# Attention softmax on score rows: one score product instead of two, exponentials in place, probabilities transposed by TensorE

## The reference

```
x = x + tanh(g_xattn) * attention(layernorm(x), ctx, mask)
    Q, K, V = projections, Q and K rotated (RoPE)
    scores  = Q K^T / sqrt(32);  scores = -inf where mask == 0
    out     = softmax(scores) V, heads joined, times W_o
x = x + tanh(g_ffn) * experts(layernorm(x))
    affinity = softmax(x gate^T);  each of 8 experts takes its top 56 rows of every batch
    out = scatter-add of gating * down(silu(gate(x)) * up(x))
```

## Time and profile before

| | us |
|---|---|
| median of 3 runs (1951.43 to 1954.47) | 1953.86 |
| profiled execution | 1952.03 |
| its span | 1950.1 |
| TensorE busy | 1816.3 (93%) |
| VectorE busy | 1020.4 (52%) |
| ScalarE busy | 717.0 (37%) |
| GpSimd busy | 213.3 (11%) |
| mean granted TensorE clock | 0.970 |

### The profile page before, as it was taken

The page is one execution under the profiler, slowest core; times in us unless marked ns, Lnnn a source line. Parts: engine busy times, 40 slices in busy tenths (PEclk is TensorE's granted clock), DMA queues, the critical chain, the costliest instruction groups (busy, mean ns, idle before and its releaser), DMA issues. The chain is left out here.

```text
span 1950.1 us, 30053 instructions
## 1 busy us (share of the span) xinstructions
PE 1816.3 (93%) x11654; PEld 1564.5 (80%) x11654; DVE 1020.4 (52%) x1650; ACT 717.0 (37%) x1134; POOL 213.3 (11%) x288
## 2 busy tenths in 40 slices
PE   7999974999999999998299999999999999999995
PEld 6989962776676676775189999999999999999995
DVE  6665643676676576574444353543535445354441
ACT  3232221444344444353044343433424334343340
POOL 0000001112122112111100020200202011020101
PEclk9999996999999999999689999999999999999998
DMA  5545446565465564551333353533535334353431
GB/s 221 192 172 204 159 151 159 135 166 140 123 171 139 125 177 134 128 152 39 113 105 109 98 147 116 137 108 99 154 108 137 114 108 136 108 145 108 120 105 19
DMA packets 77229, 257.33 MB, mean 132 GB/s; under 512 B 10824, under 2 KB 10824, under 8 KB 75856
## 3 DMA queue, kind: packets, MB, share of 16 engines
q1 hardware_dynamic: 65136, 221.92, 37.1%
q0 software_dynamic: 12000, 34.13, 7.4%
HBM read 193.39 MB, written 51.61 MB: 126 GB/s over the span
## 5 line engine op out<-in xcount | busy, mean ns | idle before, releaser
L1413 PE MATMUL gu_ps<-xs_hi,ws_hi 128*128 128x448 f32 x1024 | 372.4, 364 | 3.0 <-DVE xs_lo L1348 3.0
L1415 PE MATMUL gu_ps<-xs_hi,ws_lo 128*128 128x448 f32 x1024 | 371.9, 363 | 0.0
L1414 PE MATMUL gu_ps<-xs_lo,ws_hi 128*128 128x448 f32 x1024 | 371.0, 362 | 0.0
L786 DVE CUSTOM_DVE_ANT_0 junk<-m_ps,mq 112x752 f32<-112x752 f32 x256 | 236.1, 935 | 198.0 <-PE m_ps L1047 195.7
L1343 DVE TENSOR_TENSOR ws_lo<-w_raw,ws_hi 128x1024 fp32r<-128x1024 f32 x192 | 235.4, 1226 | 189.1 <-ACT ws_hi L1293 188.1
L671 ACT ACTIVATE e_t<-s_ps 125x448 f32<-125x448 f32 x384 | 201.1, 547 | 221.7 <-PE s_ps L1074 221.1
L1293 ACT ACTIVATE ws_hi<-w_raw 128x1024 fp32r<-128x1024 f32 x192 | 201.7, 1051 | 164.4 <-PE y_ps L1432 146.6
L1413 PEld LDWEIGHTS gu_ps<-xs_hi,ws_hi 128*128 128x128 f32 x1024 | 192.7, 188 | 15.4 <-issue 3.3
L1414 PEld LDWEIGHTS gu_ps<-xs_lo,ws_hi 128*128 128x128 f32 x1024 | 192.6, 188 | 13.5
L1415 PEld LDWEIGHTS gu_ps<-xs_hi,ws_lo 128*128 128x128 f32 x1024 | 192.8, 188 | 13.2
L1074 PE MATMUL s_ps<-qs,ks 128*125 128x224 f32 x768 | 197.8, 353 | 0.0
(11 more groups left out here) (133 smaller groups left out, 2552.0 us busy)
## 6 DMA issues: line engine op xcount, KB each, us to landing
w_raw<-wstream SPq DMA_DIRECT2D x192, 512.0 KB, 3.5
ks<-k_split SPq DMA_DIRECT2D x192, 188.0 KB, 3.8
k_split<-k_split SPq DMA_DIRECT2D x32, 752.0 KB, 3.5
v_rows<-v_out SPq DMA_DIRECT2D x16, 750.0 KB
vs<-v_rows SPq DMA_DIRECT2D x16, 750.0 KB
c_raw<-ctxT SPq DMA_DIRECT2D x7, 1500.0 KB, 12.9
qs<-q_hi POOLq DMA_DIRECT2D x64, 112.0 KB, 3.0
mq_raw<-maskq SPq DMA_DIRECT2D x8, 656.2 KB, 10.3
```

What stands on the lines that cost most here:

```text
L786: nc.vector.tensor_tensor_reduce(junk[u % 2][:].rearrange("p (a n) -> p a n", a=2), m_ps[u % 2][0:QP, :, 0:KN], mq[:, qc].rearrange("p (a ...
L1413: nc.tensor.matmul(o, w_hi[s][:, w], xs_hi[:, c], start=(c == 0), stop=False)
L1414: nc.tensor.matmul(o, w_hi[s][:, w], xs_lo[:, c], start=False, stop=False)
L1415: mm = nc.tensor.matmul(o, w_lo[s][:, w], xs_hi[:, c], start=False, stop=(c == DC - 1))
```

## The change

The second score product is gone. VectorE's instruction keeps what it used to throw away: it writes the masked scores, times minus the scale, to `sm` and their row minimum to `least`. ScalarE takes the exponential of these rows in place in SBUF, with `least` as the bias, and its instruction sums the row into `sums`. TensorE transposes the probabilities of a head (12 transposes, four for each of three PSUM tiles), and ScalarE or, in 8 of the 48 tiles of a batch, VectorE copies a tile to `e_t`. The reciprocal is now taken of 8 sums a row; GpSimd spreads it over 32 columns each, TensorE turns that, ScalarE copies it, and VectorE multiplies straight from PSUM. The matmuls with ones, the transposed mask with its load and conversion, and the extra rows of `qs` and `ks` go. The scores run three heads ahead.

TensorE's new parts, and its order in a head t:

```
-                    nc.tensor.matmul(o, identb[0:KP, 0:KP], mt[j][:, 2 * pc:2 * pc + 2, :].rearrange("p c s -> p (c s)"), start=True, stop=False)
...
+                def turn_rows(b, h, pc):
+
+                    if pc == 0:
+                        for qc in range(QC):
+                            pe.wait_ge(exp_done[qc], H * b + h + 1)
+                    n = tile_of(b, h, pc)
+                    if n >= 2:
+                        pe.wait_ge(*emptied(n - 2))
...
+                            mm = nc.tensor.transpose(t_ps[n % 2][0:KP, a:a + QP], sm[:, h % SR, qc, c * KP:c * KP + KP], ident[0:QP, 0:QP])
...
+                def turn_parts(b, q):
+
+                    after(pe, cx_done, NG * b + q)
+                    pe.wait_ge(spread_done, NG * b + q + 1)
...
+                        turn_rows(b, t, 0)
+                        next_scores(0)
+                        turn_rows(b, t, 1)
+                        next_scores(1)
+                        if t % HG:
                             last_values()
+                        turn_rows(b, t, 2)
+                        if t % HG == 0:
+                            last_parts()
```

ScalarE's:

```
+                    nc.scalar.activation(rows, rows, ACT.Exp, bias=least[:, h % KSLOTS, qc:qc + 1], scale=-1.0,
+                                         accum_out=sums[:, h // HG % 2, qc, h % HG:h % HG + 1]).then_inc(exp_done[qc], 1)
...
                         for pc in range(KC // 2):
+                            if not on_dve(t, pc):
+                                empty(b, t, pc)
+                            if pc < QC:
+                                next_exp(pc)
+                            if pc == 0 and t % HG == 1:
+                                if t > HG:
+                                    copy_parts(b, t // HG - 1)
...
+                        if t == 8 and not last:
+                            high_q(b + 1)
```

VectorE's, and the first lines of GpSimd's:

```
+DVE_SLOTS = (0, 1, 2, 4, 7, 9, 11, 13)
...
+                                mask_scores(b, t + MLEAD, qc)
...
+                            if qc == 0 and on_dve(t, DVE_TILE):
+                                empty(b, t, DVE_TILE)
+                        if t % HG == 0:
+                            if t >= 2 * HG:
+                                normalise(b, t // HG - 2)
...
+                        if t % HG == HG - 1:
+                            invert(b, t // HG)
...
+                        if t % HG == HG - 1:
+                            spread_parts(b, t // HG)
```

More of the change, by code:

```diff
@@ L405, in attend @@
         q_hi, q_lo = sb(st, "q_hi", [P, NG, S], F32R), sb(st, "q_lo", [P, NG, S], F32R)
[L406 to L407 removed]
+        sm = sb(st, "sm", [QP, SR, QC, SK])
+        least, sums = sb(st, "least", [QP, KSLOTS, QC]), sb(st, "sums", [QP, 2, QC, HG])
+        parts, spread = sb(st, "parts", [QP, 2, QC * HG]), sb(st, "spread", [QP, 2, QC, P])
         e_t = [sb(st, f"e_t{j}", [KP, KC // 2, PAIR]) for j in range(2 * HG)]
[L409 removed]
+        c_r, cx = sb(st, "c_r", [P, S]), sb(st, "cx", [P, NG, S])
         x2 = x_res
@@ L473, in hold @@
                 def hold(s_, v_):
-                    if not (isinstance(v_, int) and v_ <= 0):
+                    if v_ > 0:
                         sp.wait_ge(s_, v_)
@@ L625, in end @@
                 def end():
-                    for q in range(1, NG):
-                        normalise(B - 1, q)
                     root(B - 1, 1, 2 * B)
@@ new lines, in next_exp @@
+                        def next_exp(qc):
+                            if t + 1 < H:
+                                exp(b, t + 1, qc)
+                            elif not last:
+                                exp(b + 1, 0, qc)
+                        for pc in range(KC // 2):
+                            if not on_dve(t, pc):
[5 more added lines that the diff above has]
+                                    copy_parts(b, t // HG - 1)
+                                elif not first:
+                                    copy_parts(b - 1, NG - 1)
+                            if pc == 0 and t in (1, 2) and not last:
+                                x_columns(b + 1, t - 1)
+                            if pc == 0 and t in (12, 13) and not first:
@@ L716, in body @@
                                 x2_columns(b - 1, t - 12)
-                            if t == 15:
-                                logit_exp(b - 1)
+                        if t == 8 and not last:
+                            high_q(b + 1)
+                        if t == 15 and not first:
+                            logit_exp(b - 1)
                 def end():
-                    for q in range(2, NG):
-                        copy_ctx(B - 1, q)
+                    copy_parts(B - 1, NG - 1)
@@ L958, in end @@
                     b = B - 1
-                    for q in range(1, NG):
-                        invert(b, q)
+                    for q in (NG - 2, NG - 1):
+                        normalise(b, q)
                     residual(b, 0)
@@ L1176, in end @@
                     b = B - 1
-                    for part in range(HG):
+                    turn_parts(b, NG - 1)
+                    for part in range(HG - 1):
                         values(b, NG - 1, part)
```

342 lines of the change are left out of this document (121 added, 221 removed).

## The result

The changed kernel takes 1978.15 us (median of 4 runs, 1977.59 to 1979.66), against 1952.64 of the kernel before on the same chip (1950.43 to 1954.47): a ratio of 1.0132, 95% interval 1.0115 to 1.015, or 25.5 us slower. I forecast 1960 and slower, so the sign is right and the size (+6) is a quarter of what it should be. The time lies inside the range of 1912 to 1985, but above the 1948 to 1975 that I gave the walk itself, and I had "slower" at 0.49 only: the sign was close to a toss. Its profiled execution has a span of 1975.7 against 1950.1, at a mean granted clock of 0.959 against 0.970.

The account below looks back on a forecast made before the run. TensorE was taken to bound the kernel before. Six full batches at +2.6 us (+16), start -2, last batch -6 and last projection -2 made +6 on 1952.03: 1958, as median 1960; range 1912 to 1985.

Parts of the forecast that it names:

- the walk: Head-by-head timing of one attention batch across the engines: 75.9 us, 76.9 with small gaps, against 74.3 before.
- rival 2: TensorE bounds the attention batches throughout: 63.6 us a batch, 1880 us in all, chance 0.12.
- the gap of 1: Small TensorE idle gaps in a batch that the head-by-head timing leaves out: 1 us added to 75.9.
- the normalise: VectorE's product that TensorE waits for in heads 0, 4, 8 and 12: 4.5 us a batch together.
- the stall of the norm: Before head 15's norm, VectorE waits for GpSimd's parts copy and then the root: 2 us a batch.
- `high_q`: ScalarE's copy at the end of head 8, which VectorE's `low_q` waits for: 1 us a batch lost.
- the values behind `copy_parts`: Value matmuls of heads 1, 5, 9 and 13 wait for ScalarE's output copy: late by 0.7 us.
- all-or-nothing rival: TensorE's clock falls to 1.2 GHz between the projections: +16 us a batch, some 2060 us, chance 0.06.
- Rival 3: ScalarE's exponential costs 1.05 us instead of 0.80: +2.5 us a batch, 1980 us, chance 0.13.
- The start: Before the full batches, three heads of maxima are needed instead of five: 2 us less.
- The last batch: No masks or scores for a next batch, so no lag there: 6 us less.
- The last projection: The final output projection follows its values sooner, where it ran at a clock of 0.50: 2 us less.

Follow-up runs that it names:

- all_three: The changed kernel with VectorE's normalise ahead of the masks, GpSimd's root ahead of the spread copy, and ScalarE's copy_parts ahead of tile copy and exponential: 1913.42 us.
- before_few_ones: The kernel before, with the matmuls with ones kept for the last of six key chunks only, so row sums omit the other five: 1921.19 us.
- norm_first: The changed kernel with VectorE's normalise (product into cx) ahead of the two masks and tile copy in heads 0, 4, 8 and 12: 1958.25 us.
- norm_copy: all_three without root_first, so VectorE's norm still waits for the root behind the spread copy: 1933.69 us.
- all_high: all_three with high_q and low_q moved from the end of head 8 to the end of head 7: 1905.40 us.
- norm_root: all_three without moving ScalarE's copy_parts: 1943.41 us.
- no_read: The changed kernel with exponentials that give no row sums (sums a constant, output unnormalised), so no accumulator reads: 1964.89 us.
- root_first: The changed kernel with GpSimd taking the root of the next batch's moments before it spreads the parts in head 15: 1969.41 us.
- filler4: The changed kernel with four extra 128x512 matmuls into an unused bank ahead of turn_parts in head 0 of six batches: 1978.20 us.

## Why the prediction was right in sign and short in size

**What bounds.** TensorE's sum fell, but to 65.65 us a batch, not 61.4; at a held clock it is 64.1 (all_three). before_few_ones shows that the engines behind TensorE were close: even without new work for them only half of what is removed comes back. So rival 2, in which all that TensorE loses comes off the time, was out of reach with the order as it is. VectorE (49.1 forecast, 48.6 measured) and ScalarE (about 50; 52.2) came out near their sums, and so did the small prices: the product 0.39 us, not 0.35, the reciprocal 0.20, not 0.17, the spread copy 0.40, not 0.5.

**The walk.** It held well. Head 14 to 0: forecast 13.9, measured 13.80. Heads 8 to 13: 24.05 and 24.99. Heads 1 to 7: 37.9 and 40.01, of which 0.8 is the fall of 3.4 us in heads 0 to 2. With the gap of 1 the walk gave 76.9; the measured 78.8 less 0.8 is 78.0, and all batches but the first, less their falls, take 77.7 to 78.0. So the walk was about 1 us a batch short. No head is off by more than 0.6 us; heads 3, 10 and 11, for which I had ScalarE's exponentials bound, take 3.50, 3.57 and 3.51, not 3.15, 3.25 and 3.2. The places at which I said the cover is lost are those that the experiments found: the normalise (norm_first: waits of 60.7 us down to 11.6), the stall of the norm (2 forecast; 1.76 measured, 1.8 a batch by norm_copy against all_three) and `high_q` (1; all_high: 1.5 a batch); and the values behind `copy_parts`, which the walk had at 0.7, waited 1.03 in head 9.

**The step that failed is the clock.** I priced it as an all-or-nothing rival (the clock at 1.2 GHz between the projections, 2060, chance 0.06) and left it out of the sum. It falls once or twice in a batch for 3.4 or 6.8 us. The short fall costs 0.8 us in heads 0 to 2 and 1.7 in the q projection of head 4, which then takes 4.89 us instead of 3.21; the long one costs 2.1 in heads 0 to 2 and 2.6 in norm_copy. The batches of 81 us have a short one in head 14 and a long one in head 0, that of 79.3 two short ones, the others one. The deficit of 18.8 us is an upper bound. Holding each of the nine falls against the same heads of a batch without one gives some 12 us in all (an estimate from the starts of the heads in the trace), of 25.5 measured against 6 forecast. The prediction called itself wrong if the granted clock left 1.00 inside the loop; on this point it was wrong, and the row for it was in my hands: 3.14 us of idling, then 0.50, while the walk had TensorE idle for over 4 us in head 0. It would have priced the five falls there, not the four behind waits of 1.5 to 1.8 us. All_three has the same transposes at a clock of 1.00 throughout the six batches, and before_few_ones, which has only the few of the kernel before, has three falls behind waits of 1.9 to 2.1 us. So the rule on transposes that I quoted from the Trainium skill ("TensorE: Matmul & The Clock Gate", Part 4: PE-mode transpose) is not enough to bring a fall about here, and not needed for one. Whether transposes make the clock fall behind shorter waits is not shown: the kernel before waited 1.34 us in every batch and kept 1.00, norm_root had falls behind waits of 0.7 and 0.8.

**The exponential.** I took 0.80; it is 0.91 from start to start, 0.81 without the sum (no_read). The Trainium skill's figure for the bias ("ScalarE: Activation LUTs", What ACT_TABLE_LOAD costs; by it I had estimated 0.82) fits the latter; the read of the accumulator costs 0.10 more. Rival 3 gives the measured total, 1980, by a price (1.05) that the trace does not show: the right number for a wrong reason. The read reaches the end with 1.2 us a batch, inside the gaps that I allowed.

**The ends.** The six batches cost +30.7, not +16: 15 more, some 12 for the falls and the rest for the walk. The start gave 4.4, not 2. The last batch was to give 6 and gave nothing: from the last mask conversion to the last output projection it takes 91.53 us, before 91.59. The last projection was to give 2 by a warm clock and did not:

```profile
950.34 5.45 PE L979 MATMUL w_ps<-wo_sb,cx 128*112 128x512 f32 x8 [0.60 <-DVE cx L764]
```

5.45 us, 5.35 before. The clock was down there again, to 0.50 from 943.7 to 954.0, so the warm clock that I had priced was not there; and the last batch has a fall of 6.8 us too, at 875.4. So of the 19.6 us that the sum was short, the batches make 14.7 and the two ends 7.3 more, less the 2.4 that the start gave beyond its 2.

**What stays open.** What exactly lets the clock fall. The wait ahead of it is part of it, since taking waits away ended the falls; but root_first shortened the longest wait and had more deficit, norm_root kept all of it with waits of 0.7 to 1.2 us while all_three has waits of 1.2 us and no fall, filler4 only moved the falls, and in norm_copy the same wait had a fall in one batch and none in another. How the 65 us of all_three divide between the clock and the waits themselves is not measured either.

## What to carry to other kernels

When a change takes work from the engine that bounds, walk the new order head by head: the lengths of the heads where no fall hit them, could be read off it to 0.6 us each before anything ran. Each wait then has two prices, its own length and what a clock that falls behind it costs; look in the trace before for a place where the engine idles that long, price the clock from there, and count on some falls behind shorter waits. Small reorderings are to be tried together: here three of them gave 44 us by themselves and 65 as a set, and turned a loss of 25 us into a gain of 39.

## What the runs showed of the hardware

An exponential that also sums its row (112x752) is followed by a read of the accumulator of 194 ns, of which 0.10 us are not hidden; VectorE's read behind the mask takes 83 ns. The granted clock fell behind waits of TensorE of 1.5 to 4.1 us that the kernel before does not have in its loop, and in norm_root behind waits of 0.7 to 1.2 us, mostly for 3.4 or 6.8 us; the same order of the same instructions had the fall in one batch and not in the next (norm_copy, 75.25 and 74.71 against 72.39). A fall costs at most half of its own length: 0.8 to 1.7 us for 3.4, 2.1 to 2.6 for 6.8. Some kernels with falls scatter more: norm_first from 1952.35 to 1963.78, all_high, which has none, from 1902.72 to 1905.80; but the changed kernel, with nine falls, only from 1977.59 to 1979.66.
